# One turning of the probabilities per step in place of two, in a Perceiver layer on one core

## What is computed

```python
def _L0_xattn_ref(inputs_q, inputs_kv, Wq, Wk, Wv, Wo):
    q = (inputs_q @ Wq).reshape(b, sq, H, HD) * (1.0 / np.sqrt(HD))
    k = (inputs_kv @ Wk).reshape(b, skv, H, HD)
    v = (inputs_kv @ Wv).reshape(b, skv, H, HD)
    scores = jnp.einsum('bqhd,bkhd->bhqk', q, k)
    attn = jax.nn.softmax(scores, axis=-1)
    ctx = jnp.einsum('bhqk,bkhd->bqhd', attn, v).reshape(b, sq, H * HD)
    return ctx @ Wo
...
x = x + _L0_xattn_ref(_layernorm(x, axis=-1), ctx_2048, ...)
x = x + _L0_attn_ref(_layernorm(x, axis=-1), ...)
x = x + _L0_ffn_ref(_layernorm(x, axis=-1), ...)
```

## Time and profile before

| what | value |
|---|---|
| median of 3 runs | 2012.89 us (2012.73 to 2013.48) |
| the profiled execution, its own time | 2015.33 us |
| its span, first to last instruction | 2013.5 us |
| granted TensorE clock over the span | 0.988 |
| TensorE (PE) busy | 97% of the span |
| VectorE (DVE), ScalarE (ACT) busy | 80%, 56% |
| DMA queue 1 (all data), share of the 16 DMA engines | 76.2% |

### The profile page before, as it was taken

One profiled execution on the slowest core, in us unless ns is written; L12 is line 12 of the kernel. 1 busy time (PEld: TensorE's weight loads), 2 busy tenths in 40 slices (PEclk: granted clock), 3 DMA queues, 4 the chain that ended last, 5 costly groups with the idle time before them and its releaser, 6 DMA issues.

```text
span 2013.5 us, 46241 instructions
## 1 busy us (share of the span) xinstructions
PE 1945.6 (97%) x17330; PEld 1591.4 (79%) x17334; DVE 1605.9 (80%) x3444; ACT 1127.3 (56%) x2484; POOL 272.4 (14%) x465
## 2 busy tenths in 40 slices
PE   5789999999999999999999999999999999999896
PEld 5677887887887987987987987977978978877662
DVE  4788888787888888888888888888888888877736
ACT  3565566566665555555655555555555565655422
POOL 1011111111111111111111111111111111100000
PEclk8899999999999999999999999999999999999998
DMA  5668798788797878878887888787887787776570
GB/s 149 147 109 170 160 159 167 148 161 166 151 160 150 148 141 160 153 151 160 155 152 150 156 154 173 148 157 154 147 165 155 140 144 144 130 142 154 128 285 6
DMA packets 966944, 304.44 MB, mean 151 GB/s; under 512 B 893984, under 2 KB 952864, under 8 KB 965824
## 3 DMA queue, kind: packets, MB, share of 16 engines
q1 hardware_dynamic: 966720, 301.47, 76.2%
HBM read 72.16 MB, written 4.46 MB: 38 GB/s over the span
## 4 chain that ended last, share of the span: by engine, by line
PE 92%; DVE 5%; issue 1%; ACT 1%; DMA 0%; POOL 0%; ACTq 0%; SPq 0%; DVEq 0%; POOLq 0%
PE ps_v L1212 25%; PE ps_s L1197 25%; PE ps_t L1197 19%; PE ps_w L1212 19%; PE ps_w L1171 1%; DVE pp L880 1%; PE ps_v L1184 1%; PE ps_v L1298 1%; PE ps_t L1291 1%; PE ps_s L1340 0%; PE ps_s L1153 0%; DVE prob L875 0%; ACT bulk L609 0%; DVE bulk L816 0%; PE ps_w L1374 0%
## 5 line engine op out<-in xcount | busy, mean ns | idle before, releaser
L1197 PE MATMUL ps_s<-bulk 128*128 128x128 f16 (+2 forms) x4752 | 583.4, 272 | 2.7 <-DVE bulk L816 2.7
L1212 PE MATMUL ps_v<-nring,pt 128*128 128x256 f16 x4704 | 580.9, 273 | 1.6 <-ACT ps_w L646 0.9
L1212 PEld LDWEIGHTS ps_v<-nring,pt 128*128 128x128 f16 x4704 | 458.5, 98 | 62.0 <-DVE acc L799 2.6
L1197 PEld LDWEIGHTS ps_s<-bulk 128*128 128x128 f16 x4752 | 404.6, 98 | 114.7 <-DVE bulk L816 2.9
L1197 PE MATMUL ps_t<-bulk 128*128 128x384 f16 (+2 forms) x3564 | 454.0, 272 | 20.1 <-ACT ps_t L660 17.2
L1212 PE MATMUL ps_w<-nring,pt 128*128 128x256 f16 x3528 | 451.8, 273 | 8.1 <-DVE ps_w L899 6.4
L880 DVE SCALAR_TENSOR_TENSOR pp<-prob,pp 128x384 f16<-128x384 f32 (+4 forms) x680 | 423.4, 689 | 0.0
L1197 PEld LDWEIGHTS ps_t<-bulk 128*128 128x128 f16 x3564 | 301.8, 98 | 112.8 <-ACT ps_t L660 18.9
L1212 PEld LDWEIGHTS ps_w<-nring,pt 128*128 128x128 f16 x3528 | 340.0, 98 | 57.6 <-DVE ps_w L899 8.9
L640 ACT ACTIVATE pp<-prob 128x384 f16<-128x384 f32 (+4 forms) x680 | 370.9, 623 | 5.5 <-DVE prob L875 4.7
L629 ACT ACTIVATE prob<-ps_s,nmax 128x768 f32<-128x768 f32 (+2 forms) x136 | 119.1, 876 | 432.8 <-DVE nmax L855 426.1
(11 more groups left out here) (187 smaller groups left out, 1397.0 us busy)
## 6 DMA issues: line engine op xcount, KB each, us to landing
stage<-in_ctx SPq DMA_DIRECT2D x196, 128.0 KB, 3.0
wst<-in_w SPq DMA_DIRECT2D x64, 256.0 KB, 3.2
bulk<-in_vo SPq DMA_DIRECT2D x16, 512.0 KB, 6.1
acc<-in_qk SPq DMA_DIRECT2D x11, 512.0 KB, 4.1
pt<-pp SPq DMA_TRANSPOSE x272, 5.7
tern_d<-wter SPq DMA_DIRECT2D x32, 128.0 KB, 3.0
bulk<-tern_d SPq DMA_DIRECT2D x2, 2048.0 KB, 19.7
nring<-in_aw SPq DMA_DIRECT2D x3, 1024.0 KB, 11.3
```

The lines of the kernel that those rows point to most:

```text
L1197: ins = mm(out if n == 1 else out.rearrange("p (n m) -> p n m", m=P), q_part(e, qlo, a)[:, c * P:(c + 1) * P], t_moving(k, run, tlo, b, c) ...
L1212: ins = mm(dst, pt[:, tile:tile + P], n_part(c, clo, b), start=(first and n == 0 and plo == 0 and clo == 0), stop=(last and n == w - 1 and ...
```

## The change

The two transfers of a step become one of all fourteen pieces, with one semaphore `in_pt`. It is issued after all five low parts. The first `hi_part` of the next step and the first value product wait for it whole. To be contiguous, group 1 lies right behind group 0 in `pp` and `pt`, also in narrow windows.

```diff
         def p_at(k, g, lo=0, blk=0):
-            return (8 * WIN * P if g else 0) + (lo * (4, 3)[g] + blk) * cols(k)
+            return (8 * g + lo * (4, 3)[g] + blk) * cols(k)
...
-            def turn_p(k, g):
-                sp.wait_ge(lo_done, 5 * k + (2, 5)[g])
+            def turn_p(k):
+                sp.wait_ge(lo_done, 5 * (k + 1))
                 if k >= LAG:
                     sp.wait_ge(v4_done, k - 1)
-                at, n = p_at(k, g), (8, 6)[g] * cols(k)
-                to = pt_at(k) + at
-                sp.dma_start_transpose(pt[:, to:to + n].rearrange("p (t q) -> p t q", q=P), pp[:, at:at + n]).then_inc(in_pt[g], 16)
+                to, n = pt_at(k), 14 * cols(k)
+                sp.dma_start_transpose(pt[:, to:to + n].rearrange("p (t q) -> p t q", q=P), pp[:, 0:n]).then_inc(in_pt, 16)
...
             for k in range(1, NS + 1):
-                turn_p(k - 1, 0)
-                turn_p(k - 1, 1)
+                turn_p(k - 1)
...
             def hi_part(k, blk, n, sums):
-                g = blk // GROUP
                 for e in range(2):
                     act.wait_ge(exp_done[e], k + 1)
                 act.wait_ge(p_sum, 4 * k + sums)
                 if k:
-                    act.wait_ge(in_pt[g], 16 * k)
+                    act.wait_ge(in_pt, 16 * k)
...
             def values(k):
-                pe.wait_ge(in_pt[0], 16 * (k + 1))
+                pe.wait_ge(in_pt, 16 * (k + 1))
...
-                pe.wait_ge(in_pt[1], 16 * (k + 1))
                 pe.wait_ge(va_copied, k + 1)
```

More of the change, by code:

```diff
@@ L266, in perceiver_layer @@
         in_nt = [sem(f"in_nt{g}") for g in range(2)]
-        in_pt = [sem(f"in_pt{g}") for g in range(2)]
+        in_pt = sem("in_pt")
         in_w = [sem(f"in_w{k}") for k in range(2)]
@@ L502, in _ @@
             sp.wait_ge(s4_done, NS)
-            sp.wait_ge(in_pt[1], 16 * NS)
+            sp.wait_ge(in_pt, 16 * NS)
             sp.dma_start(diff[:, :], diff_d).then_inc(in_const, 16)
```

## The result

The kernel after takes **2048.95 us** (median of 4 runs, 2047.83 to 2051.55); beside it the kernel before took 2012.81 (4 runs, 2012.38 to 2013.48). The ratio is 1.0177, with a 95% interval of 1.0163 to 1.0192: 36 us slower. The profiled executions are 2048.84 and 2015.33 us, spans 2046.9 and 2013.5, so in them 33.4 us are to be explained.

The account below looks back on a forecast made before the run. TensorE, 97% of the span, bounds the kernel. Late transfers cost 17.5 us in tight steps, 2.5 in the others, 1 in the tail: together 21 us, so 2034 us for the median; range 2013 to 2060, forecast alone 2019 to 2060.

Parts of the forecast that it names:

- lands 8.2 to 8.5 us behind the last low part ... just in time: Undisturbed step: the single transfer lands as the next step's first high part wants it, at 8.45 to 8.56 us; nothing lost.
- an instruction fetch holds ... the transpose: DMA engines: an instruction-queue (q8) packet during the transfer delays it, by 1.0 us early, up to 2.1 us near the end.
- 65 steps are hit ... mean 1.0 us: Of 124 steps, 53% have a packet during the transfer; 0.1 us of spare leaves high parts 0.9 us late.
- tight steps 44 x 0.53 = 23, x (0.9 - 0.15) = 17.5 us: 44 steps without ScalarE idle time before copy L660: 23 are hit and pass lateness less 0.15 us to TensorE, 17.5 us.
- The other 80: 42 hits ... 2.5 us: Steps with 1.45 us of ScalarE idle time before L660: a third of the hits cost some 0.2 us each, 2.5 us.
- Tail, 1 us: Narrow steps at the end: next high part comes 6.7 us after the last full low part, 8.3 needed; 1 us counted.
- TensorE's own wait, the chunk's turning: nothing: TensorE's wait on `in_pt` and the context chunk's turning, issued 1.4 us later, are for steps later and cost nothing.
- Absorbed: Rival: spare time in 80 of 124 steps swallows the lateness; time stays the same, 2013 to 2017 us; chance 13%.
- One transfer has a cost less: Rival: the single transfer lands earlier, 6.3 us behind the last low part, covering even hits; 2013 us; chance 6%.
- Feeds on itself: Rival: lateness runs round high parts, low parts and turning; each step loses up to 1 us, 2060 to 2100 us; chance 8%.
- Faster: Rival: one TensorE wait fewer in each step lets matmuls close up by 0.04 us; some 2008 us; chance 3%.

Follow-up runs that it names:

- late_coarse: Kernel before, still two transfers, with group 0 issued only after all five low parts and every high part waiting for both groups: 2046.68 us, ratio 1.016.
- merged_room: Kernel after with `pp` of 16 pieces, one staging buffer fewer, first parts cut in two; first two high pieces needn't wait for the step before: 2028.52 us.
- its control: Kernel after with the same buffers and cuts as `merged_room`, but all high parts wait for the turning of the step before: 2058.78 us, ratio 1.0214.

## Why the prediction was right, and where it was short

The direction and the mechanism held; the loss was forecast at 21 us and is 36 between the medians, 33.4 between the profiled executions. By its own steps:

- **"lands 8.2 to 8.5 us behind the last low part ... just in time".** Right: issue 6.35 us in the median, landing 8.4; the pair took the same. Undisturbed steps lose nothing.
- **"an instruction fetch holds ... the transpose".** Right. Without a packet no landing is later than 8.45 us, and moving the packets by 32 instructions changes which steps are late, and the time of the exposed kernel alone. q8's 2.24 MB are 64 bytes for each of the 35137 instructions that the trace has for TensorE. The prediction looked at q8 alone; the q14 packets, 73 of them from 130 to 1840 us and half as large, add two late landings.
- **"65 steps are hit ... mean 1.0 us".** The total was about right, its shape wrong. Expected were some 60 waits of 0.9 us, 54 us in all; measured 50 of 1.20 us, 59.9 us. The prediction took packets as evenly spread, 0.7 us each in the middle. The 22 that start before 3.3 us cost 0.4 us at most, but for two landings at 8.88; the nine from 5.6 to 6.8 land at 9.07 to 9.98; of the 45 from 7 to 8.5, 35 are followed by the landing 1.9 to 2.6 us behind their own start, at 9.6 to 10.3, and the other ten leave it at 8.2. What tells the ten from the 35 the trace doesn't show. Fewer steps are hit, and harder: 46 land later than 9.0 us, 38 of them later than 9.5. `late_coarse`, where packets are spread wider, has just the waits that I forecast, 50 with a mean of 0.97 us, and TensorE's waits are 18.3 us.
- **"tight steps 44 x 0.53 = 23, x (0.9 - 0.15) = 17.5 us".** The count was right: 26 of the 45 tight steps from 5 to 130 (those with an L616 ahead of L657) have a wait, and 24 stalls follow them. The price was not. ScalarE's waits in them have a mean of 1.21 us (31.4 us) where 0.9 was expected, TensorE's idle time behind them is 24.5 us. Add 0.16 us for each stall, for the overlap that it takes away, which the prediction left out: 24.5 + 3.8 = 28.3 in place of 17.5. **This is the term that was mis-sized.**
- **"The other 80: 42 hits ... 2.5 us".** About right: 2.2 us of idle time in three stalls, of which the longest, 1.1 us, already lies in the tail.
- **Tail, 1 us.** 3.5. The wait was sized without a packet, and one starts 7.85 us behind that last low part. The first high part of the first narrow step waits 3.19 us for the transfer, not 1.6, and so starts at 1882.83, 9.96 us behind the last low part.
- **TensorE's own wait, the chunk's turning: nothing.** Right; no wait of TensorE for `pt<-pp` is in the view.

The rivals. *Absorbed*: the spare of the 80 steps does absorb, and the tight ones have none. *One transfer has a cost less*: it hasn't. 14 pieces land in 8.4 us, 4 + 10 in 8.5, 8 + 6 in 8.3. The Trainium skill (DMA: Bandwidth & Descriptors, section Rules for kernel authors) has it that small transfers should be coalesced; for these transposes, issued back to back on one queue, no run shows a gain of more than 0.1 us from it. The rule names 64 KB, and these transfers are far above it: 24 and 18 tiles of 128x128 in half precision are 786 and 590 KB. *Feeds on itself*: no. The spare of the steps in between takes the lateness up. Late landings do occur in a row, up to five (steps 5 to 9, 57 to 61), but each of them has a packet of its own that starts 5.6 us or more behind the last low part. *Faster*: no row for it.

That waits through ScalarE carry most of the loss is shown by `merged_room` against its control (30.3 us); that it doesn't need the merging as such, by `late_coarse` (32.9 us, with an interval that overlaps that of the kernel after).

## What to carry to other kernels

Before two transfers are merged, look at both ends of each: when the earlier one could start, and which reader could start on a part. Here each of these two spares alone held the loss to some 3 us of 2013, and giving up both cost 33. A transfer that is "just in time" in an undisturbed step is late in practice, by the delays that the trace shows for it (up to 2 us here), in the steps in which something else uses the DMA engines near its end. And where a wait can't be shortened, look for a piece of the waiting engine's work that doesn't need it, and follow what is queued behind: 0.47 us moved in front gave some 5 us, 1.68 us moved in front gave the stall to VectorE.

## What was not expected of the hardware

- A q8 packet of 16 KB that starts in the first 3.3 us of a 42-tile transpose is caught up almost whole (20 of 22 land by 8.56 us). Of the 40 that start 7.5 to 8.2 us in, 32 land it about 2 us behind the packet's own start, at 9.8 to 10.3 us in place of 8.2 to 8.4; eight do nothing to it.
- A q14 packet, of 8 KB, can do the same: two of them, at 7.85 and 8.02 us, landed it at 9.2 and 9.4 us.
- The packets' places are those of the program, most of them to half a microsecond and on two chips, and a transpose holds some of them back: cutting the one transfer in 4 and 10 pieces moved nine of them forward by 2 to 4 us.
- So the kernel after depends on the length of TensorE's program. 32 instructions ahead of all other work made it some 9 us slower, with 51 late landings, of which only 33 are in steps that were late before; on the kernel before they made 0.05%, which can't be told from nothing.
- Transposes issued back to back on one queue show one tail: 8.4 us for one of 42 tiles, 8.5 for 12 and 30.
